# Attention inside a four-block network: score banks, exponentials and pair sums rearranged

## The chip, the cores and the metric

The kernel runs on one core of a Trainium2 chip. The metric is the device time of one execution in microseconds (us), the median over several runs.

## What is computed

The reference is a chain of blocks on 16 images of 128 channels and 32 x 32 pixels: a grouped convolution with batch normalisation, a linear attention, a compositional softmax attention, a feed-forward mixture, a second attention, and a routed mixture. The change touches only the third, which the kernel calls `phase_attn`. Cut to what matters it is

```python
sq = (x @ wq_s).reshape(b, n, S, DH).transpose(0, 2, 1, 3) * scale   # S=8 heads, DH=16, n=1024
sk = (x @ wk_s).reshape(b, n, S, DH).transpose(0, 2, 1, 3)
rv = (x @ wv_r).reshape(b, n, R, DH).transpose(0, 2, 1, 3)           # R=2
search_attn = softmax(einsum('bsid,bsjd->bsij', sq, sk), axis=-1)
retrieved = einsum('bsij,brjd->bsird', search_attn, rv)
retrieval_sim = einsum('bsid,bsird->bsir', rq, retrieved @ wk_ret)
out = einsum('bsir,bsird->bsid', softmax(retrieval_sim, -1), retrieved)
t = t + out.transpose(0, 2, 1, 3).reshape(b, n, S * DH) @ w_out
```

So there are 16 batches x 8 heads x 1024 x 1024 scores. Each gets an exponential; the exponentials are multiplied by values and also summed for the denominators.

## The kernel before

**Tiling.** For each batch, `STEPS` = 32 steps k run over query half (512 queries), quad of heads (4 of the 8) and block j of 128 keys: k = 8 g + j, with g = 2 half + quad. Step k has four scores (one per head of the quad, 128 keys x 512 queries, bf16 operands of 99 rows, L1508), four exponentials into the tile `P[k % 4]`, and four value products (L1535, float32, 32 rows of the bank `num` each, added up over the 8 steps of g). The denominators take half the products: GpSimd adds the tiles of an even step and the odd step behind it into `pairs` (L1410), and TensorE multiplies `pairs` by ones into the bank `den` (`totals`, L1546), once per two steps.

**Side work.** The scores need a maximum per query that is folded into the operands beforehand. While batch b is worked on, TensorE makes the scores of batch b+1 a second time with queries as rows (`max`, L1480, four per step) into a ring of three `side` banks, and VectorE reduces each (L1599). The same ring carries the odd jobs at fixed steps: `rows` (the maxima turned into operand rows, steps 1 and 17), `tokens` (L1492, numerators and denominators transposed to tokens, four times at steps 2 to 5 for the second half of the batch before and 18 to 21 for the first half of this one; VectorE copies them to `numT` and `recT`), `back` (steps 5 and 22) and `wout` (L1502, steps 6 and 23). `side_work(k, first, last)` returns the list of a step, odd jobs ahead of the maxima, and each unit waits until VectorE has emptied the bank three units back.

**The order on TensorE** is written out by hand, in `slot` (L1555 on). In step k: the fourth score of step k+1, the first quarter of the side work (one unit of four or five), scores 0 and 1 of step k+2 into the two-bank tile `Spair`, the middle of the side work (two units of four), on even k the totals, score 2 of step k+2 into the bank `Sone`, the rest of the side work, then the values of step k. `Sone` is one bank for scores 2 and 3, so score 3 waits until score 2's exponential is done, and score 2 of the next step until score 3's is.

**ScalarE** (`exps`, L1664 on) does one 1024-wide exponential of `Spair` (L1670) and two 512-wide ones of `Sone` (L1675) per step. At steps 8, 16, 24 and 0 of the next batch it has to empty `num` between them (`save`, L1685), and one step later `den` (L1688): `exps(b, k + 1, saved)` does it right behind the first exponential. The save of `num` waits for the last value product of the eight.

**GpSimd** (`pair`, L1405) waits for `den_done` of the pair sum before, since `pairs` is one tile, and for the exponentials of both its steps. Between pair sums it does `retrieve` in seven parts (L1411 on): behind pair sums 10 to 15 and pair sum 0 of the next batch for the first half, behind pair sums 2 to 8 for the second. Part 0 (L1423) waits for the last `tokens` of its half.

**SyncE** loads operands of later batches when the score counter `s_ready` says that a batch, or its first 24 steps, are through. The batches 0, 1, 14 and 15 are written out; 2 to 13 are a hardware loop over two batches a pass (`over`, L931).

Of the kernel before, what the change touches and what calls it, by code (L numbers as in the profile page):

```python
# [13 lines left out]
ALU = mybir.AluOpType  # L14
# [1193 lines left out]
STEPS = 32  # L1208
MAX_UNITS = 128
QUAD = 4  # L1210
SLOTS = 4
SIDES = 3
TOKENS_AT = (2, 18)
# [35 lines left out]
def phase_attn(nc, K, D, X):  # L1249
# [6 lines left out]
    with Mem(nc, "at") as m:  # L1256
        qo = [m.sb(f"qo{u}", [KM, SH, N], BF16) for u in range(2)]
        ko = [m.sb(f"ko{u}", [KM, SH, N], BF16) for u in range(2)]
        pairs = m.sb("pairs", [C, QUAD, CH])
# [3 lines left out]
        numT = [m.sb(f"numT{h}", [C, 4, 2 * C]) for h in range(2)]  # L1263
        recT = [m.sb(f"recT{h}", [C, 32]) for h in range(2)]
# [12 lines left out]
        Spair = m.ps("Spair", [C, 2, CH])  # L1277
        Sone = m.ps("Sone", [C, CH])
# [60 lines left out]
        with nc.Block() as block:  # L1339
            @block.sync  # L1340
            def _(sp):
# [31 lines left out]
                def slot(b, u, last):  # L1373
                    if not last and not is_first(b):

                        sp.wait_ge(s_ready, 96 * b)
                        load(b + 1, 1 - u, 1)
# [13 lines left out]
                    if not isinstance(b, int) or b < B - 2:  # L1391

                        sp.wait_ge(s_ready, 96 * b + 72)
                        load(b + 2, u, 0)
# [6 lines left out]
            def _(g):  # L1401
# [3 lines left out]
                def pair(b, i):  # L1405

                    wait_if(g, den_done, 16 * b + i)
                    g.wait_ge(p_ready, 96 * b + 6 * i + 6)
                    a = 2 * i % SLOTS
                    g.tensor_tensor(pairs[:, :, :], P[a][:, :, :], P[a + 1][:, :, :], ALU.add).then_inc(pair_done, 1)  # L1410

                def retrieve(b, h, part, tokens):
# [4 lines left out]
                    nv = numT[h][:, :, :].rearrange("p i (s r d) -> p (i s) r d", r=RH, d=DH)  # L1417
                    pv = prod[:, :, :].rearrange("p i (s r d) -> p (i s) r d", r=RH, d=DH)
                    rec = recT[h]
# [23 lines left out]
                    elif part == 5:  # L1443
                        step(g.tensor_tensor(heads, numT[h][:, :, :].rearrange("p i (s d) -> p (i s) d", d=DH),
# [24 lines left out]
            def _(pe):  # L1469
# [34 lines left out]
                def score(b, u, k, i, out):  # L1504
                    g, j = divmod(k, 8)
                    half, quad = divmod(g, 2)
                    h = QUAD * quad + i
                    return pe.matmul(out, ko[u][:, h, j * C:(j + 1) * C], qo[u][:, h, half * CH:(half + 1) * CH],  # L1508
                                     start=True, stop=True)

                def scores01(b, u, k):

                    wait_if(pe, p_ready, 96 * b + 3 * k - 2)
                    if k in (0, 8):
                        pe.wait_ge(row_in[u][k // 8], rows_count(b, u))
                    score(b, u, k, 0, Spair[:, 0, :])
                    score(b, u, k, 1, Spair[:, 1, :]).then_inc(s_ready, 1)

                def scores2(b, u, k):
                    wait_if(pe, p_ready, 96 * b + 3 * k)  # L1520
# [1149 lines left out]
```

## Time and profile before

| What | Value |
|---|---|
| Median of 3 runs | 5345.9 us (5343.29 to 5345.98) |
| The profiled execution: its own time | 5344.89 us |
| The profiled execution: span on the chip | 5343.3 us |
| Mean granted TensorE clock over the span | 0.908 |
| Attention phase, first score to last value product | about 2007 us |

The span is what the profiler saw of the execution, and 1.6 us lie around it. Durations below are from that one execution. PE is TensorE's matmul part, PEld its weight loads, DVE VectorE, ACT ScalarE, POOL GpSimd; a bracket at the end of a row of a timeline is the time the engine was idle before it and whose signal ended that. Matmuls overlap: one that is listed with 0.39 us gives way to the next after about 0.22 us, so starts are read, not lengths. `x8` at a value or total product is four float32 products of two passes each.

### The profile page before, as it was taken

What the parts mean: (1) busy time and instruction counts of PE and PEld (TensorE: products, weight loads), DVE (VectorE), ACT (ScalarE), POOL (GpSimd) and SP (SyncE); (2) the same over time, 40 slices, a digit from 0 to 9 for tenths busy, and PEclk for the clock granted to TensorE, in tenths of its full rate; (3) what the DMA queues carried; (4) which work ended last, traced back from release to release, by engine and by line L of the source; (5) the groups of instructions that cost most, each with busy time, mean ns of one, the idle gap of its engine ahead of it and who ended that gap; (6) DMA issues with size and microseconds to landing.
All of it is one profiled execution on the core that took longest, in us unless ns stands there. A gap on an engine that the chain in (4) does not pass through costs nothing. (4 is left out here: it accounts for less than half of the span.)

```text
span 5343.3 us, 71207 instructions
## 1 busy us (share of the span) xinstructions
PE 4422.3 (83%) x21775; PEld 1685.3 (32%) x21775; DVE 3064.3 (57%) x5454; ACT 2100.1 (39%) x3333; POOL 1821.6 (34%) x1328
## 2 busy tenths in 40 slices
PE   5499999994699999999999999976999999565323
PEld 2133333332422222222222222223444444343222
DVE  4777777764687776767677767624000000567562
ACT  3311111114526555556565555653344433413100
POOL 1000000003727776767676767772000000303001
PEclk9799999997969999999999999987999999866655
DMA  1343444424822222222222222011000000213204
GB/s 68 74 99 88 93 104 89 97 59 172 249 29 30 32 30 30 39 31 33 30 30 30 38 31 35 8 37 46 0 0 0 0 0 0 99 43 121 80 0 137
DMA packets 208208, 295.43 MB, mean 55 GB/s; under 512 B 43943, under 2 KB 136109, under 8 KB 206525
## 3 DMA queue, kind: packets, MB, share of 16 engines
q1 hardware_dynamic: 179768, 256.87, 21.7%
q10 hardware_dynamic: 23808, 25.17, 1.3%
q0 software_dynamic: 4368, 10.07, 0.6%
q8 instruction: 142, 2.33, 0.2%
q14 instruction: 122, 1.00, 0.1%
HBM read 94.49 MB, written 69.73 MB: 31 GB/s over the span
## 5 line engine op out<-in xcount | busy, mean ns | idle before, releaser
L1599 DVE TENSOR_REDUCE at_mx<-at_side 128x1 f32<-128x512 f32 x2048 | 1307.2, 686 | 387.1 <-PE at_side L1480 339.9
L1410 POOL TENSOR_TENSOR at_pairs<-at_P 128x2048 f32<-128x2048 f32 x256 | 1159.7, 4530 | 588.6 <-PE at_den L1546 475.0
L1675 ACT ACTIVATE at_P<-at_Sone 128x512 f32<-128x512 f32 x1024 | 611.5, 597 | 608.2 <-PE at_Sone L1508 607.4
L1480 PE MATMUL at_side<-at_ko,at_qo 96*128 96x512 bf16 x2048 | 716.8, 397 | 55.6 <-DMA at_ko<-qk 23.3
L1670 ACT ACTIVATE at_P<-at_Spair 128x1024 f32<-128x1024 f32 x512 | 523.7, 1023 | 217.8 <-PE at_Spair L1508 173.9
L1952 ACT ACTIVATE ff_hs<-ff_ph,ff_b 128x512 f32<-128x512 f32 x512 | 351.7, 687 | 525.0 <-PE ff_ph L1922 525.0
L1535 PE MATMUL at_num<-at_P,at_rvt 128*32 128x512 f32 x4096 | 546.7, 606 | 0.0
L1922 PE MATMUL ff_ph<-ffn_Y,ff_w 128*128 (+1 forms) x1024 | 525.3, 595 | 8.6 <-DMA ff_b<-in_b_dram 8.6
L1936 PE MATMUL ff_po<-ff_hs,ff_w2s 128*128 128x512 f32 x1024 | 522.9, 592 | 0.0
L616 PE MATMUL la_acc<-la_rep,la_wagg 128*32 128x512 f32 x4096 | 511.1, 606 | 1.1 <-DMA la_rep<-la_pad 1.1
L1971 DVE SCALAR_TENSOR_TENSOR X<-ff_po,ffn_b2w,X 128x512 f32 (+1 forms) x32 | 24.0, 751 | 823.5 <-PE ff_po L1936 823.5
L773 DVE SCALAR_TENSOR_TENSOR la_dwq<-la_pad,la_taps,la_dwq 128x1024 f32<-128x1024 f32 x384 | 491.6, 1280 | 7.2
L1508 PE MATMUL at_Sone<-at_qo,at_ko 99*128 99x512 bf16 x1024 | 399.7, 390 | 107.0 <-ACT at_P L1675 94.5
L1008 POOL TENSOR_TENSOR n_ln_ab<-n_ln_mv,eps 128x4 f32<-128x4 f32 x96 | 19.1, 199 | 1201.2 <-DVE n_ln_mv L999 1199.7
L587 POOL DMA_DIRECT2D proj<-la_y x32 | 17.4, 544 | 996.2 <-ACT la_y L847 996.2
L1508 PEld LDWEIGHTS at_Sone<-at_qo,at_ko 99*128 99x128 bf16 x1024 | 98.1, 96 | 783.9 <-ACT at_P L1675 489.8
L1480 PEld LDWEIGHTS at_side<-at_ko,at_qo 96*128 96x128 bf16 x2048 | 200.4, 98 | 372.6 <-DVE at_mx L1599 148.4
L1508 PE MATMUL at_Spair<-at_qo,at_ko 99*128 99x512 bf16 x1024 | 309.1, 383 | 0.0
L1546 PE MATMUL at_den<-at_pairs,ones 128*32 128x512 f32 x2048 | 278.0, 615 | 5.9 <-POOL at_pairs L1410 5.6
L1922 PEld LDWEIGHTS ff_ph<-ffn_Y,ff_w 128*128 128x128 f32 x1024 | 195.4, 191 | 254.2 <-issue 245.0
L1936 PEld LDWEIGHTS ff_po<-ff_hs,ff_w2s 128*128 128x128 f32 x1024 | 194.9, 190 | 245.4 <-issue 244.9
L1023 ACT ACTIVATE n_ln_xt<-n_ln_front,n_ln_ab 128x128 f32<-128x128 f32 x384 | 144.3, 456 | 103.2 <-POOL n_ln_ab L1014 93.5
(412 smaller groups left out, 4848.6 us busy)
## 6 DMA issues: line engine op xcount, KB each, us to landing
la_rep<-la_pad SPq DMA_DIRECT2D x512, 162.2 KB, 3.6
qk<-ap_part SPq DMA_DIRECT2D x32, 768.0 KB, 3.7
at_qo<-qk SPq DMA_DIRECT2D x192, 128.0 KB, 4.6
at_ko<-qk SPq DMA_DIRECT2D x192, 128.0 KB, 7.3
n_ln_xs<-X SPq DMA_DIRECT2D x96, 256.0 KB, 2.3
u<-ap_us SPq DMA_DIRECT2D x32, 320.0 KB, 4.0
X<-in_x_dram SPq DMA_DIRECT2D x4, 2048.0 KB, 21.7
proj<-la_y POOLq DMA_DIRECT2D x32, 256.0 KB, 2.3
```

Source lines behind the costliest of these rows:

```text
L616: last = pe.matmul(acc[h][32 * j:32 * j + 32, :], wagg[:, p - 1, j, g, :], view[:, :, 0:HW], start=(g == 0), stop=(g == NG - 1))
L773: v.scalar_tensor_tensor(out, image, taps[:, t:t + 1], out, ALU.mult, ALU.add).then_inc(tap_done, 1)
L1410: g.tensor_tensor(pairs[:, :, :], P[a][:, :, :], P[a + 1][:, :, :], ALU.add).then_inc(pair_done, 1)
L1480: return pe.matmul(side[bank][:, :], qo[1 - u][0:KQ, s, i * C:(i + 1) * C], ko[1 - u][0:KQ, s, h * CH:(h + 1) * CH], start=True, stop=True)
L1508: return pe.matmul(out, ko[u][:, h, j * C:(j + 1) * C], qo[u][:, h, half * CH:(half + 1) * CH], start=True, stop=True)
L1535: last = pe.matmul(num[32 * i:32 * i + 32, :], rvt[u][:, j, :], P[k % SLOTS][:, i, :], start=(j == 0), stop=(j == 7))
L1599: v.reduce_max(mx[:, n // 2, n % 2:n % 2 + 1], side[bank][:, :], AX.X).then_inc(side_saved, 1)
L1670: a.activation(P[k % SLOTS][:, 0:2, :], Spair[:, :, :], ACT.Exp).then_inc(p_ready, 1)
L1675: a.activation(P[k % SLOTS][:, 2 + i, :], Sone[:, :], ACT.Exp).then_inc(p_ready, 1)
L1922: pe.matmul(ph[j % R][:, :], w1[:, f, :], Y[:, bass.ds(b * N + half * CH, CH)], start=True, stop=True).then_inc(h_mm, 1)
L1936: done = pe.matmul(po[half][:, :], w2s[u][:, f, :], hs[j % R][:, :], start=(f == 0), stop=(f == FT - 1)).then_inc(h_used, 1)
L1952: a.activation(hs[j % R][:, :], ph[j % R][:, :], ACT.Gelu, bias=b1[:, j % FT:j % FT + 1]).then_inc(h_ready, 1)
```

## The change

The scores go into a ring `S` of three single banks, one after another: head number n = 4 k + i uses bank n % 3, and waits for the exponential of the head that had the bank before (n - 3; at the start of a batch, where the ring breaks off since 128 is not a multiple of 3, the heads one or two before). Every score raises `s_ready` and every exponential is 512 wide and raises `p_ready`, so both count 128 (`HEADS`) per batch where they counted 96. In step k TensorE now issues scores 0, 1, 2 and 3 of step k+2, each followed by a quarter of the side work, with the totals behind the second. The saves on ScalarE stand ahead of the third exponential. `pairs` becomes two tiles used in turn, so that a pair sum waits for the totals of the pair sum two back. `numT` and `recT` become one tile each, and the first copy into them waits for part 5 of the other half's `retrieve`. `tokens` move from steps 2 to 5 and 18 to 21 to steps 3 to 6 and 19 to 22. PSUM still holds eight banks (three side, three score, `num`, `den`). The diff without what only renames:

```diff
-STEPS = 32
 MAX_UNITS = 128
...
 SLOTS = 4
+STEPS = 32
 SIDES = 3
-TOKENS_AT = (2, 18)
+RING = 3
+HEADS = STEPS * 4
+TOKENS_AT = (3, 19)
 BACK_AT = (5, 22)
...
         ko = [m.sb(f"ko{u}", [KM, SH, N], BF16) for u in range(2)]
-        pairs = m.sb("pairs", [C, QUAD, CH])
+        pairs = [m.sb(f"pairs{u}", [C, QUAD, CH]) for u in range(2)]
         P = [m.sb(f"P{u}", [C, QUAD, CH]) for u in range(SLOTS)]
...
         sums = m.sb("sums", [C, 4, CH])
-        numT = [m.sb(f"numT{h}", [C, 4, 2 * C]) for h in range(2)]
-        recT = [m.sb(f"recT{h}", [C, 32]) for h in range(2)]
+        numT = m.sb("numT", [C, 4, 2 * C])
+        recT = m.sb("recT", [C, 32])
         ub = [m.sb(f"ub{h}", [C, 4, C]) for h in range(2)]
...
         side = [m.ps(f"side{u}", [C, CH]) for u in range(SIDES)]
-        Spair = m.ps("Spair", [C, 2, CH])
-        Sone = m.ps("Sone", [C, CH])
+        S = [m.ps(f"S{u}", [C, CH]) for u in range(RING)]
         num = m.ps("num", [C, CH])
...
-                        sp.wait_ge(s_ready, 96 * b)
+                        sp.wait_ge(s_ready, HEADS * b)
                         load(b + 1, 1 - u, 1)
...
-                        sp.wait_ge(s_ready, 96 * b + 72)
+                        sp.wait_ge(s_ready, HEADS * b + 96)
                         load(b + 2, u, 0)
...
-                    wait_if(g, den_done, 16 * b + i)
-                    g.wait_ge(p_ready, 96 * b + 6 * i + 6)
+                    wait_if(g, den_done, 16 * b + i - 1)
+                    g.wait_ge(p_ready, HEADS * b + 8 * i + 8)
                     a = 2 * i % SLOTS
-                    g.tensor_tensor(pairs[:, :, :], P[a][:, :, :], P[a + 1][:, :, :], ALU.add).then_inc(pair_done, 1)
+                    g.tensor_tensor(pairs[i % 2][:, :, :], P[a][:, :, :], P[a + 1][:, :, :], ALU.add).then_inc(pair_done, 1)
...
                     heads = prod[:, :, :].rearrange("p i (s d) -> p (i s) d", d=DH)
-                    nv = numT[h][:, :, :].rearrange("p i (s r d) -> p (i s) r d", r=RH, d=DH)
+                    nv = numT[:, :, :].rearrange("p i (s r d) -> p (i s) r d", r=RH, d=DH)
                     pv = prod[:, :, :].rearrange("p i (s r d) -> p (i s) r d", r=RH, d=DH)
-                    rec = recT[h]
+                    rec = recT
                     if part == 0:
...
                     elif part == 5:
-                        step(g.tensor_tensor(heads, numT[h][:, :, :].rearrange("p i (s d) -> p (i s) d", d=DH),
+                        step(g.tensor_tensor(heads, numT[:, :, :].rearrange("p i (s d) -> p (i s) d", d=DH),
                                              sim[:, :, :].rearrange("p s (r o) -> p (s r) o", o=1).to_broadcast([C, 64, DH]),
...
-                def score(b, u, k, i, out):
+                def score(b, u, k, i):
                     g, j = divmod(k, 8)
                     half, quad = divmod(g, 2)
-                    h = QUAD * quad + i
-                    return pe.matmul(out, ko[u][:, h, j * C:(j + 1) * C], qo[u][:, h, half * CH:(half + 1) * CH],
-                                     start=True, stop=True)
-
-                def scores01(b, u, k):
-
-                    wait_if(pe, p_ready, 96 * b + 3 * k - 2)
-                    if k in (0, 8):
-                        pe.wait_ge(row_in[u][k // 8], rows_count(b, u))
-                    score(b, u, k, 0, Spair[:, 0, :])
-                    score(b, u, k, 1, Spair[:, 1, :]).then_inc(s_ready, 1)
-
-                def scores2(b, u, k):
-                    wait_if(pe, p_ready, 96 * b + 3 * k)
-                    score(b, u, k, 2, Sone[:, :]).then_inc(s_ready, 1)
-
-                def scores3(b, u, k):
-                    pe.wait_ge(p_ready, 96 * b + 3 * k + 2)
-                    score(b, u, k, 3, Sone[:, :]).then_inc(s_ready, 1)
+                    h, n = QUAD * quad + i, 4 * k + i
+
+                    wait_if(pe, p_ready, HEADS * b + (n - 2 if n >= RING else n - 1 if n < 2 else -2))
+                    if k in (0, 8) and i == 0:
+                        pe.wait_ge(row_in[u][quad], rows_count(b, u))
+                    pe.matmul(S[n % RING][:, :], ko[u][:, h, j * C:(j + 1) * C], qo[u][:, h, half * CH:(half + 1) * CH],
+                              start=True, stop=True).then_inc(s_ready, 1)
...
                         wait_if(pe, num_saved, 4 * b + g)
-                    pe.wait_ge(p_ready, 96 * b + 3 * k + 3)
+                    pe.wait_ge(p_ready, HEADS * b + 4 * k + 4)
                     for i in range(QUAD):
...
                     for i in range(QUAD):
-                        last = pe.matmul(den[32 * i:32 * i + 32, :], K["ones"][:, 0:32], pairs[:, i, :],
+                        last = pe.matmul(den[32 * i:32 * i + 32, :], K["ones"][:, 0:32], pairs[(k // 2 - 1) % 2][:, i, :],
                                          start=(j == 0), stop=(j == 6))
...
                     if first:
-                        scores01(b, u, 0)
-                        scores2(b, u, 0)
-                        scores3(b, u, 0)
-                        scores01(b, u, 1)
-                        scores2(b, u, 1)
+                        for n in range(8):
+                            score(b, u, n // 4, n % 4)
                     for k in range(STEPS):
...
                         work = side_work(k, first, last)
-                        cuts = [0, (len(work) + 1) // 4, (3 * len(work) + 1) // 4, len(work)]
-                        if k + 1 < STEPS:
-                            scores3(b, u, k + 1)
-                        elif not last:
-                            scores3(b + 1, 1 - u, 0)
                         ahead_of = (b, u, k + 2) if k + 2 < STEPS else None if last else (b + 1, 1 - u, k + 2 - STEPS)
-                        for part in range(3):
-                            for w in work[cuts[part]:cuts[part + 1]]:
+                        for i in range(QUAD):
+                            if ahead_of:
+                                score(*ahead_of, i)
+                            for w in work[(i * len(work) + 2) // 4:((i + 1) * len(work) + 2) // 4]:
                                 fill(w, b, u, side_free(b, at), at % SIDES).then_inc(side_ready, 1)
                                 at += 1
-                            if part == 0 and ahead_of:
-                                scores01(*ahead_of)
-                            if part == 1 and k % 2 == 0 and not (first and k == 0):
+                            if i == 1 and k % 2 == 0 and not (first and k == 0):
                                 totals(b, k)
-                            if part == 1 and ahead_of:
-                                scores2(*ahead_of)
                         values(b, u, k)
...
                         if n == 0:
-                            wait_if(v, out_ready, 2 * b - 1 - h)
-                        v.tensor_copy(numT[h][:, n, :], side[bank][:, 0:2 * C])
-                        v.reciprocal(recT[h][:, 8 * n:8 * n + 8], side[bank][:, 2 * C::32]).then_inc(side_saved, 1)
+                            wait_if(v, post_step, 11 * (2 * b - 1 - h) + 10)
+                        v.tensor_copy(numT[:, n, :], side[bank][:, 0:2 * C])
+                        v.reciprocal(recT[:, 8 * n:8 * n + 8], side[bank][:, 2 * C::32]).then_inc(side_saved, 1)
                     elif kind == "back":
...
                         wait_if(a, pair_done, 16 * b + k // 2 - 1)
-                    a.wait_ge(s_ready, 96 * b + 3 * k + 1)
-                    a.activation(P[k % SLOTS][:, 0:2, :], Spair[:, :, :], ACT.Exp).then_inc(p_ready, 1)
-                    if saved:
-                        save(*saved)
-                    for i in range(2):
-                        a.wait_ge(s_ready, 96 * b + 3 * k + 2 + i)
-                        a.activation(P[k % SLOTS][:, 2 + i, :], Sone[:, :], ACT.Exp).then_inc(p_ready, 1)
+                    for i in range(QUAD):
+                        if saved and i == 2:
+                            save(*saved)
+                        a.wait_ge(s_ready, HEADS * b + 4 * k + i + 1)
+                        a.activation(P[k % SLOTS][:, i, :], S[(4 * k + i) % RING][:, :], ACT.Exp).then_inc(p_ready, 1)
```

## Rows read from the trace of the kernel before

**Rows 1.** The page, busy time of each engine over the whole span.
```profile
PE 4422.3 (83%) x21775; PEld 1685.3 (32%) x21775; DVE 3064.3 (57%) x5454; ACT 2100.1 (39%) x3333; POOL 1821.6 (34%) x1328
```

**Rows 2.** Stretches, busy us (count) of PE, PEld, DVE, ACT, POOL, then TensorE clock, DMA.
```profile
1544.00:3551.60 2007.60, 1865.80 (x10838) 537.05 (x10837) 1383.58 (x2410) 1191.44 (x1756) 1444.38 (x626) 0.99 0.20 29
2339.40:2464.60 125.20, 117.97 (x690) 34.44 (x690) 92.09 (x161) 74.90 (x111) 91.28 (x41) 1.00 0.23 32
```

**Rows 3.** The page, costliest groups: the attention's own on DVE, POOL and ACT.
```profile
L1599 DVE TENSOR_REDUCE at_mx<-at_side 128x1 f32<-128x512 f32 x2048 | 1307.2, 686 | 387.1 <-PE at_side L1480 339.9
L1410 POOL TENSOR_TENSOR at_pairs<-at_P 128x2048 f32<-128x2048 f32 x256 | 1159.7, 4530 | 588.6 <-PE at_den L1546 475.0
L1675 ACT ACTIVATE at_P<-at_Sone 128x512 f32<-128x512 f32 x1024 | 611.5, 597 | 608.2 <-PE at_Sone L1508 607.4
...
L1670 ACT ACTIVATE at_P<-at_Spair 128x1024 f32<-128x1024 f32 x512 | 523.7, 1023 | 217.8 <-PE at_Spair L1508 173.9
```

**Rows 4.** Timeline of TensorE, steps 28 and 29 of a batch.
```profile
2542.94 0.39 PE L1508 MATMUL at_Sone<-at_qo,at_ko 99*128 99x512 bf16 x1
...
2543.38 0.60 PE L1508 MATMUL at_Spair<-at_qo,at_ko 99*128 99x512 bf16 x2
...
2544.34 1.06 PE L1546 MATMUL at_den<-at_pairs,ones 128*32 128x512 f32 x8
2545.34 0.39 PE L1508 MATMUL at_Sone<-at_qo,at_ko 99*128 99x512 bf16 x1
...
2545.88 1.07 PE L1535 MATMUL at_num<-at_P,at_rvt 128*32 128x512 f32 x8
2546.88 0.39 PE L1508 MATMUL at_Sone<-at_qo,at_ko 99*128 99x512 bf16 x1
...
2548.72 1.07 PE L1535 MATMUL at_num<-at_P,at_rvt 128*32 128x512 f32 x8
2549.72 0.39 PE L1508 MATMUL at_Sone<-at_qo,at_ko 99*128 99x512 bf16 x1
```

**Rows 5.** Timeline, end of step 7 and start of step 8.
```profile
2464.59 1.07 PE L1535 MATMUL at_num<-at_P,at_rvt 128*32 128x512 f32 x8
2465.80 0.58 ACT L1685 COPY at_sums<-at_num 128x512 f32<-128x512 f32 x1 [0.95 <-PE at_num L1535]
...
2466.28 0.60 ACT L1675 ACTIVATE at_P<-at_Sone 128x512 f32<-128x512 f32 x1
...
2466.94 0.39 PE L1508 MATMUL at_Sone<-at_qo,at_ko 99*128 99x512 bf16 x1 [1.28 <-ACT at_P L1675]
```

**Rows 6.** Waits of TensorE over the whole attention: us in total, times, longest.
```profile
PE at_Sone L1508 <- ACT at_P L1675: 94.5, 73, 6.5
```

**Rows 7.** Timeline, steps 5 and 6 of a batch, which carry the odd jobs.
```profile
2453.57 0.60 PE L1492 MATMUL at_side<-ident,at_sums 128*128 128x128 f32 x4
...
2454.55 0.20 DVE L1628 RECIPROCAL at_recT<-at_side 128x8 f32<-128x8 f32 x1
...
2456.56 2.36 POOL L1423 TENSOR_TENSOR at_prod<-at_numT,at_ub 128x1024 f32<-128x1024 f32 x1
2456.75 1.06 PE L1535 MATMUL at_num<-at_P,at_rvt 128*32 128x512 f32 x8
...
2459.27 1.02 PE L1480 MATMUL at_side<-at_ko,at_qo 96*128 96x512 bf16 x3
```

**Rows 8.** Timeline, last batch: two pair sums, and two scores through one bank.
```profile
3538.29 4.53 POOL L1410 TENSOR_TENSOR at_pairs<-at_P 128x2048 f32<-128x2048 f32 x1 [0.36 <-PE at_den L1546]
...
3544.05 4.54 POOL L1410 TENSOR_TENSOR at_pairs<-at_P 128x2048 f32<-128x2048 f32 x1 [0.26 <-PE at_den L1546]
...
3545.19 0.39 PE L1508 MATMUL at_Sone<-at_qo,at_ko 99*128 99x512 bf16 x1
...
3546.27 0.39 PE L1508 MATMUL at_Sone<-at_qo,at_ko 99*128 99x512 bf16 x1 [0.26 <-ACT at_P L1675]
```

**Rows 9.** Timeline of TensorE, first instruction of a new pass of the batch loop.
```profile
2562.26 0.60 PE L1508 MATMUL at_Sone<-at_qo,at_ko 99*128 99x512 bf16 x1 [5.70 <-issue]
```

## The prediction

> **What bounds the kernel now.** I read the page first: TensorE is busy 83% of the span, the other engines 34 to 57% [rows 1]. The chain that ended last is the tail of the last block and says nothing of the attention, so I cut that phase out: 2007.6 us, in which TensorE is busy 1865.80, VectorE 1383.58, GpSimd 1444.38, ScalarE 1191.44, at a granted clock of 0.99, the level of 2.4 GHz [rows 2]. One batch is 125.20 us. No engine but TensorE is near its limit, and the large idle times of the others behind it (608.2 us of ScalarE before scores, 475.0 of GpSimd before totals [rows 3]) are theirs, not the kernel's. So the question is where TensorE stands still.
>
> The timeline answers it. From start to start, an even and an odd step without odd jobs take 2546.88 - 2542.94 = 3.94 us and 2549.72 - 2546.88 = 2.84 us [rows 4]. A score or maximum gives way after 0.22, a value or total product after 1.00, and each change to float32 costs some 0.09: 8 x 0.22 + 1.00 + 0.09 = 2.84 and 1.09 more for the totals. These steps have no stall. At 32 steps they would make 16 x 6.78 = 108.5 us; the odd jobs (8 `tokens` and 2 `back` at 0.44, 2 `wout` at 0.86, 2 `rows` at 0.22) about 6.6 more. That is 115.1 of 125.2, so only some 10 us per batch are open at all.
>
> More than half of it is the save of `num`. Values of step 7 start at 2464.59, so the next score could start at 2465.59. ScalarE has to wait for these values, saves at 2465.80, starts the exponential behind it at 2466.28, and only its end frees `Sone`: the score starts at 2466.94, 1.35 us late [rows 5]. Four of these per batch are 5.4 us. The wait of TensorE on this line is 94.5 us in the phase [rows 6]. The rest are `rows` (twice 1.3, bound by VectorE's chain of four) and steps with `tokens`, `back` and `wout`.
>
> **The ring and the saves.** The work of TensorE stays: the same 2048 scores in a phase of 512 steps, the same side units, the same products. What moves is the order. After the change step 7 issues all of step 9's scores, of which two exponentials stand before the save and two behind it. Step 8 begins with the score of head 40, which needs the exponential of head 37: done before the save. A maximum follows, then at 0.44 head 41, which needs the exponential of head 38, the first behind the save. That ends at the same moment as now, so head 41 starts 1.35 after the step's start: stall 0.91 instead of 1.35 [rows 5]. The second exponential behind it starts one rhythm of 0.48 later (save to exponential in rows 5), long before its bank is wanted behind the totals. Gain 0.44 each, not 1.35. Of the 64 saves, 1 has no successor, 5 fall on the loop's turn, where TensorE stands 5.70 us for its own instructions [rows 9], and 3 are in the last batch (below): 55 x 0.44 = 24.2 us.
>
> **The exponentials.** The split costs ScalarE 2 x 597 - 1023 = 171 ns per step [rows 3], 88 us in all, bringing its 1191 to about 1280 of 2007 [rows 2]: hidden, and the end moves by nothing. What counts is latency. One bank passed on from score to score takes 1.08 us (3545.19 to 3546.27) [rows 8]. In the ring the closest pair is head 0 and head 3 of an odd step: 3 scores, 3 maxima between starts, 6 x 0.22 = 1.31. That is exactly the distance at which score 3 and score 2 stand now in the odd step that has no stall [rows 4]. Margin 0.23; if this cover were gone, each 0.1 us would cost 25.6 over 256 odd steps. The row's slope is (1023 - 597)/512 = 0.83 ns an element and leaves 0.17 us fixed. The Trainium skill (ScalarE: Activation LUTs, Rules for kernel authors) budgets about 0.3 us per activation plus 0.83 ns per element. By that estimate the exponential would be 0.72 and the bank's passage 1.21, still under 1.31: the margin would shrink and the sum stay.
>
> **One more wait and one more signal per step on TensorE.** Score 0 had no signal, score 1 no wait. Maxima, which have both, and the pair of scores, which has them once, keep the same 0.22 [rows 4], so I take 0; the upper bound is 0.09, the gap that a change to float32 shows, 46 us over 512 steps. The Trainium skill (TensorE: Matmul & The Clock Gate, The cost: per-tile semaphore tail) speaks against the change: an increment on every matmul serialises at about 26 ns. By it the estimate would be 512 x 26 ns = 13 us less gain; no row shows such a step.
>
> **Two pair tiles.** GpSimd may start a pair sum when both steps' exponentials are there, half a us before the even step, instead of behind its totals, about 3 us earlier. TensorE waits for it nowhere in the loop, so this gives 0 there. What it covers: part 0 of `retrieve` now waits for `tokens` in step 6 or 22. Token start to reciprocal's end is 1.18 (2453.57 to 2454.75) and part 0 takes 2.36 [rows 7]: in step 6, 0.22 + 1.18 + 0.1 + 2.36 = 3.9, then the pair sum of 4.53 [rows 3] ends at 8.4. Steps 6 (3.94 + 0.44 + 0.86) and 7 take 5.24 + 2.84 = 8.08, and the exponential that overwrites its tile is queued behind the save, at 9.7; totals at 9.9. Slack over 1 us, cost 0. In step 22 the slack is larger, with `back` and `wout` in the steps.
>
> **Moved odd jobs.** `tokens` move by one step; two of each half stay in odd steps. Step 5 (`tokens`, `back`) is bound by VectorE's emptying now, 3.18 us from tokens to values (2453.57 to 2456.75) [rows 7]; with the last maxima spread out I get 3.01. In step 6 the third maximum of a row of three waits 0.20 for `wout`'s bank (1.02 instead of 0.82 [rows 7]); in the new order it comes behind the totals. With some 0.1 elsewhere, 0.5 per batch x 14 = 7.0 us; bounds 0 and 14. The single `numT` waits for part 5, which ends a step and more before. SyncE's thresholds mark the same heads; queue waits there cost 0.
>
> **The last batch** has no maxima. Its pair sums follow each other at 5.76 (3538.29 to 3544.05) [rows 8]: sum, totals, sum, one tile. With two it is TensorE: odd step 1.08 + 0.22 + 1.09 = 2.39, even 3.94 - 4 x 0.22 = 3.06, 5.45 in all. 15 x 0.31 less GpSimd's `retrieve`, which then nearly fills it: 3 us, bounds 0 and 8.
>
> **Sum.** 24.2 + 7.0 + 3 = 34. The profiled execution is 5344.9, so 5311; the median is 1.0 above it: 5312.
>
> **Rivals.**
> 1. The save's stall goes wholly, because the score that waits finds other work ahead of it. For: the ring has one bank more ahead. Against: TensorE issues in order and head 41 is third in its row. 5346 - 55 x 1.35 - 10 = 5262. Chance 0.06.
> 2. The ring gains nothing: the stall is only moved, the jobs' gain is eaten by waits on `tokens`, within 10 us of 5346. For: the order is new in all 512 steps. Chance 0.13.
> 3. Slower: the passage of a bank from head 0 to head 3 in odd steps is longer than 1.31, since ScalarE's four small exponentials run closer behind one another. Price 256 us per us over; it decides from 1.31 + 34/256 = 1.44 on. At 1.54 it is 59 - 34 = 25 slower, 5371. For: margin 0.23 only. Against: 1.08 measured, and the same distance stands unstalled today. Chance 0.12.
> 4. The added wait and signal do cost something on TensorE, a part of the gap of 0.09: at 0.03 a step 15 us, so 5327, still faster. For: no row has four signalled scores in a step. Against: signalled maxima keep 0.22. Chance 0.09. The page's rule on increments, above, is this mechanism at its own price.
> The forecast itself, 5300 to 5322: 0.60.
>
> **Numbers.** Faster by over 0.2% (under 5335; 10.7 us is about what can be told from no change): 0.60 + 0.06 + 0.09 = 0.75; within: 0.13; slower: 0.12. The range leaves out rival 1 and rival 3: 5280 to 5350.
>
> **What would show it.** TensorE's wait on the scores at steps 8, 16, 24 and 0 about 0.9, between the first maximum and the second score; these steps 4.85 instead of 5.29; clean steps still 3.94 and 2.84; GpSimd's wait for totals gone; pairs in the last batch under 5.76. Wrong would be odd steps above 2.84, TensorE waiting for pair sums at steps 8 or 24, or ScalarE waiting for them.

## The result and the profile after

The changed kernel takes 5306.68 us (median of 4, 5304.48 to 5312.56) against 5345.34 for the one before: a ratio of 0.993, with a 95% interval of 0.9917 to 0.9943. It is 38.7 us faster; 34 were forecast and the range held.

The page of the changed kernel, busy time and the attention's groups (the columns as in [rows 3]):

```profile
PE 4422.0 (83%) x21774; PEld 1678.8 (32%) x21775; DVE 3041.7 (57%) x5454; ACT 2105.6 (40%) x3845; POOL 1822.3 (34%) x1328
...
L1652 ACT ACTIVATE at_P<-at_S 128x512 f32<-128x512 f32 x2048 | 1120.2, 599 | 749.5 <-PE at_S L1513 698.1
L1411 POOL TENSOR_TENSOR at_pairs<-at_P 128x2048 f32<-128x2048 f32 x256 | 1160.3, 4533 | 316.1 <-ACT at_P L1652 295.5
```

The stretch from the first score to the last value product (columns as in [rows 2]):

```profile
1544.00:3516.70 1972.70, 1870.26 (x10833) 530.27 (x10832) 1361.35 (x2409) 1193.81 (x2263) 1446.35 (x626) 0.98 0.21 29
```

The busy times beside [rows 1] and [rows 2] are nearly the same: 1865.80 and 1870.26 us of TensorE, 1444.38 and 1446.35 of GpSimd. What became shorter is the time in which TensorE stands. GpSimd's wait for totals, 475.0 us in [rows 3], is gone from its row, and that by itself says nothing of the time, as the experiments show.

Waits of TensorE in the changed kernel, without the end of the last batch (total, times, longest; `DVEq` is the part of VectorE that issues its instructions); the first line answers to [rows 6]:

```profile
PE at_S L1513 <- ACT at_P L1652: 76.0, 77, 5.4
PE at_side L1481 <- DVEq L1601: 13.0, 29, 0.5
```

94.5 us have become 76.0. The timeline at the end of step 7 and the start of step 8, which answers to [rows 5], shows where:

```profile
2321.09 1.06 PE L1524 MATMUL at_num<-at_P,at_rvt 128*32 128x512 f32 x8
2322.09 0.39 PE L1513 MATMUL at_S<-at_qo,at_ko 99*128 99x512 bf16 x1
2322.30 0.59 ACT L1662 COPY at_sums<-at_num 128x512 f32<-128x512 f32 x1 [1.54 <-PE at_num L1524]
...
2323.44 0.39 PE L1513 MATMUL at_S<-at_qo,at_ko 99*128 99x512 bf16 x1 [0.74 <-ACT at_P L1652]
...
2323.98 1.06 PE L1535 MATMUL at_den<-at_pairs,ones 128*32 128x512 f32 x8
```

Step 8 begins at 2322.09 without a wait. The second score starts at 2323.44, 1.35 us behind it, as the stalled score in [rows 5] did; but a score and a maximum have been issued meanwhile. The late moment is the same, but more of the row's work has been issued before it, so 0.44 us less of TensorE's time is lost.

For the rest I took from the timelines of both kernels the start of every group of value products (L1535 before, L1524 after). The distance between two of them is the length of a step. The median over six batches away from the loop's turn, in us:

| Steps | Before | After |
|---|---|---|
| clean odd, clean even | 2.84, 3.94 | 2.85, 3.95 |
| 8 and 24; 16 | 5.29; 5.21 | 4.86; 4.78 |
| 1 to 6 together | 26.16 | 25.36 |
| 17 to 23 together | 28.87 | 28.40 |
| last batch, 31 steps | 94.4 | 95.3 |
| turn of the loop, over a clean batch (mean of 5) | 6.7 | 9.1 |

From the first to the last value product the profiled executions take 1998.4 and 1967.2 us: the attention gave 31.2 of the 38.7. The remainder is outside. The first value product starts at 1552.18 in the profile before and 1547.67 in the one after, and over the profiles of all kernels of this study, which share every line up to there, it moves between 1543.7 and 1552.2. The last two rows of the table took back some 13 us: 5 turns at 2.4, and 0.9 in the last batch.

### The profile page after: what moved, and what is told of

Read it like the earlier page. It is cut to its first block and busy times, and to the rows that moved or that the text cites. A ratio compares the mean times of both kernels' runs of the same rounds, so it can differ in the third digit from the quotient of the medians.

```text
span 5305.1 us, 72474 instructions
## 1 busy us (share of the span) xinstructions
PE 4422.0 (83%) x21774; PEld 1678.8 (32%) x21775; DVE 3041.7 (57%) x5454; ACT 2105.6 (40%) x3845; POOL 1822.3 (34%) x1328
## 5 line engine op out<-in xcount | busy, mean ns | idle before, releaser
L1652 ACT ACTIVATE at_P<-at_S 128x512 f32<-128x512 f32 x2048 | 1120.2, 599 | 749.5 <-PE at_S L1513 698.1
L1513 PE MATMUL at_S<-at_qo,at_ko 99*128 99x512 bf16 x2048 | 784.2, 387 | 76.0 <-ACT at_P L1652 76.0
L1481 PE MATMUL at_side<-at_ko,at_qo 96*128 96x512 bf16 x2048 | 788.8, 398 | 44.0 <-DMA at_ko<-qk 23.3
L1524 PE MATMUL at_num<-at_P,at_rvt 128*32 128x512 f32 x4096 | 550.1, 609 | 0.0
L1513 PEld LDWEIGHTS at_S<-at_qo,at_ko 99*128 99x128 bf16 x2048 | 196.1, 97 | 884.0 <-ACT at_P L1652 684.2
L1535 PE MATMUL at_den<-at_pairs,ones 128*32 128x512 f32 x2048 | 277.1, 613 | 7.7 <-POOL at_pairs L1411 7.6
L616 PEld LDWEIGHTS la_acc<-la_rep,la_wagg 128*32 128x32 f32 x4096 | 105.8, 108 | 246.5 <-issue 228.1
L831 ACT COPY la_agg<-la_acc 128x512 f32<-128x512 f32 x64 | 37.5, 587 | 343.1 <-PE la_acc L616 343.1
```

The lines of the kernel that those rows point to most:

```text
L616: last = pe.matmul(acc[h][32 * j:32 * j + 32, :], wagg[:, p - 1, j, g, :], view[:, :, 0:HW], start=(g == 0), stop=(g == NG - 1))
L1481: return pe.matmul(side[bank][:, :], qo[1 - u][0:KQ, s, i * C:(i + 1) * C], ko[1 - u][0:KQ, s, h * CH:(h + 1) * CH], start=True, stop=True)
L1513: pe.matmul(S[n % RING][:, :], ko[u][:, h, j * C:(j + 1) * C], qo[u][:, h, half * CH:(half + 1) * CH], start=True, stop=True).then_inc(s_r ...
L1524: last = pe.matmul(num[32 * i:32 * i + 32, :], rvt[u][:, j, :], P[k % SLOTS][:, i, :], start=(j == 0), stop=(j == 7))
L1535: last = pe.matmul(den[32 * i:32 * i + 32, :], K["ones"][:, 0:32], pairs[(k // 2 - 1) % 2][:, i, :], start=(j == 0), stop=(j == 6))
L1652: a.activation(P[k % SLOTS][:, i, :], S[(4 * k + i) % RING][:, :], ACT.Exp).then_inc(p_ready, 1)
```

## The experiments

Each kernel differs from the changed kernel or from the one before by the lines shown. The ratio is that to runs of the kernel before taken beside them, with its 95% interval. Those runs had medians of 5342.4 to 5343.9, against 5345.34 beside the changed kernel, so a difference in time to the changed kernel is good to some 3 us; the lengths of steps are steadier.

**1. The save one exponential earlier** (save_second).

```diff
-                        if saved and i == 2:
+                        if saved and i == 1:
```

> The changed kernel with one edit: ScalarE saves num and den ahead of the second exponential of the four instead of the third. Theory A (the stall at steps 8, 16, 24 and 0 is the score whose bank is emptied by the first exponential behind the save; its size is 1.35 us less the place of that score in TensorE's row): that score is then the first of the row (place 0 instead of 0.44), so these steps go from 4.86 back to about 5.29 and the time from 5306.7 to 5306.7 + 55 x 0.44 = 5331. Rival B (the changed kernel gained there because exponentials are shorter and the totals stand earlier, wherever the save is): no change, 5307.

Measured 5338.69 (5334.56 to 5341.4), ratio 0.9989 (0.9979 to 0.9999). Steps 8 and 24 take 5.35, steps 16 and 32 5.28; nothing else in a clean batch moved. Its timeline at step 8:

```profile
2330.29 1.06 PE L1524 MATMUL at_num<-at_P,at_rvt 128*32 128x512 f32 x8
2331.50 0.59 ACT L1662 COPY at_sums<-at_num 128x512 f32<-128x512 f32 x1 [2.03 <-PE at_num L1524]
...
2332.64 0.39 PE L1513 MATMUL at_S<-at_qo,at_ko 99*128 99x512 bf16 x1 [1.28 <-ACT at_P L1652]
```

The first score of step 8 now waits, 1.35 us from 2331.29 again. Nearly the whole gain of the change is gone, with ring, pair tiles and narrow exponentials all in place. Rival B falls. The loss is 32.0 us where 24 were expected: the save steps are 0.49 longer instead of 0.43, and the last batch, which I had left out, is 2.1 longer.

**2. The save one exponential later** (save_fourth).

```diff
-                        if saved and i == 2:
+                        if saved and i == 3:
```

> The changed kernel with one edit: ScalarE saves num and den ahead of the fourth exponential. Theory A: the score that waits for it is then the third of the row, behind the totals (place 1.96, after the 1.35), so the stall goes wholly: steps 8, 16, 24 and 0 fall from 4.86 to 3.94, and the time to 5306.7 - 55 x 0.91 = 5257. Rival B (what stands behind the save is late anyhow, so another wait takes the place): less than a third of it, over 5290.

Measured 5267.24 (5265.57 to 5271.72), ratio 0.986 (0.9844 to 0.9877): 39.4 us less than the changed kernel. The save steps take 3.94 and 3.95, and 4.06 at step 32. The timeline at step 8 has the same save and no stall:

```profile
2302.05 1.07 PE L1524 MATMUL at_num<-at_P,at_rvt 128*32 128x512 f32 x8
2303.05 0.39 PE L1513 MATMUL at_S<-at_qo,at_ko 99*128 99x512 bf16 x1
2303.26 0.59 ACT L1662 COPY at_sums<-at_num 128x512 f32<-128x512 f32 x1 [1.06 <-PE at_num L1524]
...
2303.49 0.38 PE L1513 MATMUL at_S<-at_qo,at_ko 99*128 99x512 bf16 x1
...
2304.02 1.06 PE L1535 MATMUL at_den<-at_pairs,ones 128*32 128x512 f32 x8
```

Of the expected 50, 39.4 came. Clean batches lost 3.1 us each, but at the turn of the loop a batch costs 10.3 over a clean one instead of 9.1, and step 10 has become 0.18 longer.

**3. The totals earlier instead of the save later** (totals_first).

```diff
-                            if i == 1 and k % 2 == 0 and not (first and k == 0):
+                            if i == 0 and k % 2 == 0 and not (first and k == 0):
```

> The changed kernel with one edit: on even steps the totals stand behind the first score and its maximum instead of behind the second. Theory A: head 1 of the row is then at place 1.5, past the 1.35, so the stall of 0.91 at the four save steps goes as it does in save_fourth, though the save stays where it is: 5257. It needs the pair sum 0.44 us plus earlier; the trace has it ready by 0.2 us or more at step 8. Rival B: the pair sum is late at steps 8 and 24 and TensorE waits for it instead, 5280 or more. Rival C (ScalarE itself is what is late): 5307.

Measured 5281.2 (5278.7 to 5282.43), ratio 0.9885 (0.9868 to 0.9901). Steps 8 and 24 fall to 3.98 and 3.95 though the save was not touched, so theory A holds for these steps a third time, from TensorE's side. The time is not the 5257 of theory A, though, but the one named for rival B, whose mechanism came at other steps: TensorE's waits of that kernel now have a line for pair sums.

```profile
PE at_S L1513 <- ACT at_P L1652: 31.1, 9, 5.6
...
PE at_den L1535 <- POOL at_pairs L1411: 10.0, 28, 1.3
```

They are at steps 10 and 26 (4.42 and 4.25 instead of 3.94), behind the second part of `retrieve`, not at 8 and 24. Steps 4, 6, 20 and 22 are 0.09 longer each as well.

**4. The unit `rows` behind the maxima** (rows_last).

```diff
-        if k == ROWS_AT[1]:
-            work.append(("rows", 1))
...
-        if k == ROWS_AT[0]:
-            work.append(("rows", 0))
         work += [("max", n) for n in range(QUAD * k, QUAD * k + QUAD)]
+        if k == ROWS_AT[0]:
+            work.append(("rows", 0))
+    if post and k == ROWS_AT[1]:
+        work.append(("rows", 1))
```

> The changed kernel with one edit: at steps 1 and 17 the unit rows stands behind the four maxima instead of ahead of them. Theory A (these steps take 4.3 us instead of 3.1 because VectorE's chain of four holds one of three side banks and VectorE itself, with four maxima behind it): the chain then runs beside the value products, and both steps fall by about 1.1: 5306.7 - 2 x 1.1 x 14 = 5276. Rival B (the chain is only moved into the next step, whose maxima then wait): no change, 5307.

Measured 5280.12 (5277.57 to 5280.85), ratio 0.988 (0.9864 to 0.9897). Steps 1 and 17 fall from 4.39 to 3.10; the next step is 0.18 longer. The wait on `DVEq` above, 29 times, is not in this kernel's list. Rival B is right for 0.18 of 1.29.

**5. The place of the save in the kernel before** (old_save_last).

```diff
-                    if saved:
-                        save(*saved)
                     for i in range(2):
+                        if saved and i == 1:
+                            save(*saved)
```

> The kernel before, with its double bank and its single one, and one edit: ScalarE saves num and den ahead of the third exponential (the second 512-wide one) instead of the second. Theory A (the place of the save alone makes the stall, the ring is not needed for it): the score that waits for the exponential behind the save is then the third of the next row, behind the totals, so steps 8, 16, 24 and 0 fall from 5.3 to 3.94 and the time by 55 x 1.3 = 72 from 5345: 5273, well under the changed kernel. Rival B (one single bank for two scores can't take a save without the ring): the save delays the fourth score instead, over 5320.

Measured 5274.32 (5269.24 to 5278.86), ratio 0.9869 (0.9853 to 0.9886). Steps 8, 16 and 24 take 3.94. This one edit of the old kernel is worth 68 us, more than the whole change:

```profile
2311.31 1.06 PE L1535 MATMUL at_num<-at_P,at_rvt 128*32 128x512 f32 x8
2311.47 0.59 ACT L1675 ACTIVATE at_P<-at_Sone 128x512 f32<-128x512 f32 x1
2312.31 0.39 PE L1508 MATMUL at_Sone<-at_qo,at_ko 99*128 99x512 bf16 x1
2312.52 0.58 ACT L1685 COPY at_sums<-at_num 128x512 f32<-128x512 f32 x1 [0.46 <-PE at_num L1535]
```

The exponential that frees `Sone` has started before the save, and the score at 2312.31 does not wait. The ring was not needed to take this stall away, and as built it took away a third of it.

**6. One pair tile in the changed kernel** (one_pair_tile). The tile, its wait (`16 * b + i`) and its uses are those of the kernel before.

```diff
-        pairs = [m.sb(f"pairs{u}", [C, QUAD, CH]) for u in range(2)]
+        pairs = m.sb("pairs", [C, QUAD, CH])
...
-                    wait_if(g, den_done, 16 * b + i - 1)
+                    wait_if(g, den_done, 16 * b + i)
```

> The changed kernel with one tile for the pair sums instead of two, each sum waiting for the totals of the sum before. Theory A (the second tile buys nothing in the loop): clean steps and save steps as in the changed kernel (2.85, 3.94, 4.86), only the last batch 3 us longer: 5307 to 5310. Rival B (the second tile is what lets the moved tokens and the pair sums stand side by side): TensorE waits at steps 8, 10, 24 and 26, over 5320.

Measured 5312.3 (5308.73 to 5317.36), ratio 0.9941 (0.9925 to 0.9958). The time lies between the two forecasts, 5.6 us above the changed kernel. All steps of a clean batch agree with the changed kernel within 0.02, and the last batch takes 97.5 instead of 95.3. Rival B falls: in the steps of the loop the second tile is worth nothing, and in the last batch 2.2 us.

**7. The other half of the change alone, in the kernel before** (old_two_pairs). Two pair tiles, one `numT` and `recT`, `tokens` at 3 and 19, with the old banks, order and exponentials.

```diff
-TOKENS_AT = (2, 18)
+TOKENS_AT = (3, 19)
...
-                    wait_if(g, den_done, 16 * b + i)
+                    wait_if(g, den_done, 16 * b + i - 1)
```

> The kernel before, its score banks, order on TensorE and exponentials as they were, with the other half of the change alone: two pair tiles, one numT and recT, tokens one step later. Theory A (this half is worth nothing in the loop): 5340 to 5350, save steps still 5.3, with GpSimd's wait for totals gone. Rival B (it is worth part of the 39 us): under 5335.

Measured 5341.4 (5334.54 to 5342.45), ratio 0.9993 (0.9984 to 1.0003): no difference. GpSimd's largest waits in it:

```profile
POOL at_pairs L1410 <- ACT at_P L1675: 356.0, 126, 88.2
POOL at_prod L1423 <- DVE at_recT L1628: 141.7, 31, 4.8
```

The 475 us of waiting for totals of [rows 3] have become waiting for exponentials and for `tokens`. GpSimd was not what the loop waited for; only the name of its releaser changed. The steps say that two small things cancel in the time: steps 1 to 6 and 17 to 23 fall by 0.36 per batch together, and the last batch rises from 94.4 to 97.1.

**8. `tokens` back at 2 and 18 in the changed kernel** (tokens_early).

```diff
-TOKENS_AT = (3, 19)
+TOKENS_AT = (2, 18)
```

> The changed kernel with tokens back at steps 2 and 18. Steps 2 to 6 and 18 to 23 became 0.8 and 0.45 us shorter per batch in the changed kernel. Theory A (that comes from the order in a step, scores between the side units): the sum of these steps stays within 0.1 per batch, and the last batch is 3 us shorter, since GpSimd no longer waits 4.6 us for tokens there: 5303. Rival B (it comes from the move): 1.0 per batch is lost, 5320.

Measured 5299.73 (5294.63 to 5306.39), ratio 0.9917 (0.99 to 0.9933). Steps 1 to 6 and 17 to 23 together take 53.63 against 53.76 (55.03 before the change), so what these steps gained comes from the order within a step. With `tokens` at the same steps as in the kernel before, it lies at steps 3, 5 and 6 (0.21, 0.43 and 0.21) and 19, 21 and 22 (0.21, 0.21 and 0.09). The last batch takes 89.6 instead of 95.3. GpSimd's waits in the last batch, first the changed kernel, then this one:

```profile
POOL at_prod L1424 <- DVE at_recT L1607: 7.6, 2, 4.6
```

```profile
POOL at_prod L1424 <- DVE at_recT L1607: 0.6, 2, 0.4
```

**9. The 1024-wide exponential split, alone, in the kernel before** (old_split).

```diff
-                    a.activation(P[k % SLOTS][:, 0:2, :], Spair[:, :, :], ACT.Exp).then_inc(p_ready, 1)
+                    a.activation(P[k % SLOTS][:, 0, :], Spair[:, 0, :], ACT.Exp)
+                    a.activation(P[k % SLOTS][:, 1, :], Spair[:, 1, :], ACT.Exp).then_inc(p_ready, 1)
```

> The kernel before with one edit: the 1024-wide exponential of the double bank as two 512-wide ones behind one another, with the same waits and the same signal behind the second. Theory A (the narrower exponentials are hidden and follow one another at 0.49 us, so that ScalarE's busy time hardly grows): clean steps stay 2.84 and 3.94, ScalarE's busy time in the phase 1190 to 1210, time within 5 us of 5342. Rival B (four exponentials per step cost on the path, 0.17 us each): odd steps over 2.9. On the turn of the batch loop: it cost the old order 6.9 us over a clean batch and the ring 9.1. If that comes from the longer list of instructions on ScalarE, it is 8 or more here, and the time 5 to 8 us longer; if it comes from TensorE's order or its waits, 6.9 stays.

Measured 5344.68 (5338.12 to 5349.43), ratio 1.0002 (0.9993 to 1.0012). All steps as before. The stretch of the attention:

```profile
1544.00:3551.00 2007.00, 1864.39 (x10837) 536.68 (x10835) 1383.31 (x2409) 1222.26 (x2265) 1445.76 (x626) 0.99 0.20 29
```

ScalarE has some 510 more instructions and 31 us more busy time than in [rows 2], a little over the 1190 to 1210 expected. The turn of the loop costs 6.8 us, so four exponentials a step instead of three are not what made it 9.1. This kernel still has three waits and three signals per step on ScalarE, where the ring has four.

**10 and 11. Together.** `save_fourth_rows_last` has the edits of 2 and 4, `three_edits` that of 8 as well.

> The changed kernel with both edits, the save ahead of the fourth exponential and rows behind the maxima. They gave 39.4 and 26.6 us alone and lie in different steps: if they add up, 5306.7 - 66 = 5241. If GpSimd or VectorE becomes the bound in between, less: over 5250.

> The changed kernel with three edits: save ahead of the fourth exponential, rows behind the maxima, tokens at steps 2 and 18. The first two together gave 5227.7; tokens_early shortened the last batch from 95.3 to 89.6 us. If that holds here too: 5222. If rows at step 1 and tokens at step 2 get into each other's way (the step behind rows is 0.18 longer already): 5227 or more.

Measured 5227.73 (5227.58 to 5231.53), ratio 0.9787 (0.9771 to 0.9804), and 5219.48 (5217.62 to 5223.82), ratio 0.977 (0.9754 to 0.9786). The first is 13 us better than the sum of its parts. By the steps the parts just add up: a clean batch falls by 5.4, and by 3.1 and 2.3 with each alone. The phase falls by 75.6 (1967.2 to 1891.6) against 40.7 + 30.7 = 71.4, so most of the 13 lies outside the attention. In the second the step behind `rows` is 4.56 long, 0.18 over one with `tokens` alone, and the last batch 88.2. It is the fastest of all, 87 us under the changed kernel.

**12. The two edits in the kernel before** (old_save_rows), those of 5 and 4.

> The kernel before with its double bank, and two edits: the save ahead of the third exponential and rows behind the maxima. The first gave 68 us. Theory A (rows is VectorE's chain, the same in both orders): 1.1 us less at steps 1 and 17, 27 to 34 less than 5274: 5240 to 5247. Against 5227.7 of the ring with the same two edits, the ring's own order would be worth 12 to 20 us. Rival B (with three maxima in one row the chain is in the way again): over 5260.

Measured 5254.71 (5245.9 to 5258.84), ratio 0.9832 (0.9815 to 0.9848). Steps 1 and 17 fall to 3.15, but the step behind them rises from 4.40 to 4.92, so half a microsecond of 1.24 comes back: neither theory is wholly right. A clean batch takes 118.8 against 117.0 of the ring with the same two edits. What is left of the change beside these two edits is worth 1.8 us per batch; in the times it is 27 us, of which the phase, first to last value product, shows 20.9 (1912.5 against 1891.6). Since the split exponentials (9) and the second pair tile (6, 7) gave nothing in the loop's steps, these 1.8 are the ring with its order and the moved `tokens`. Against `three_edits`, which has `tokens` at the same steps as this kernel, it is 2.1 per batch and 35 us in the times.

## Why the prediction was right

**Where TensorE stands** was read rightly: clean steps at 2.84 and 3.94 have no stall, and but for steps 10 and 26 in experiments 2, 3 and 10 they kept their length to 0.01 in every kernel of the study. One reading was wrong without harm to the sum: the gap of 0.09 is not that of a change to float32. In the trace before, value products, totals and `rows` (32 columns of weights, `128*32`) start 0.31 to 0.32 us behind a score or maximum, but the float32 products of `tokens`, `back` and `wout` (`128*128`) 0.22 to 0.23, like a bf16 one.

**The saves** were the term that carried the sum, 55 x 0.44 = 24.2. The steps gave 0.43 each, and a stall of 0.91 was left, as forecast, at the place forecast. That the stall is 1.35 less the place of the waiting score is shown by moving the save both ways (1, 2), by moving the totals (3) and in the old order (5).

**The exponentials** were right in cost (9: nothing). A term beside the sum was wrong: I let ScalarE's busy time grow by 88 us; it grew by 2. Two 512-wide exponentials behind one another are listed at 1.09 us, not at twice 0.60, so a row's mean length is not what one of a series costs. The estimate from the Trainium skill (ScalarE: Activation LUTs, Rules for kernel authors) of 0.72 for one was not what the trace showed: 0.599. The page's 0.3 us is for an activation whose bias is an operand in memory, and these have none.

**The added wait and signal** cost nothing that a step shows: 2.85 against 2.84, at most 0.01 x 512 = 5 us. By the figure of the Trainium skill (TensorE: Matmul & The Clock Gate, The cost: per-tile semaphore tail) I had estimated 0.026; the page gives it as a tail behind matmuls that each increment a semaphore, and used as a cost per step it is not borne out. The step lengths leave nothing of rival 4.

**Two pair tiles** were right at 0 in the loop (6, 7).

**The moved jobs** were put at 0.5 per batch and gave 0.80 + 0.47 = 1.27: the mechanism was right and the size too small. I worked out step 5 as 0.17 and it gave 0.44. I had followed only one side bank. My reading, which no run separates, is that with the even spacing VectorE has emptied a bank before it is wanted again. That the move itself is not the cause is shown by 8, where these steps gain 1.40 without it; in the old order the move gives 0.36 (7).

**The last batch** was the step that failed: `+3`, measured -0.9. I let GpSimd's `retrieve` nearly fill it and did not ask what the later `tokens` do there. Part 0 waits for them 4.6 us, and with no maxima between the scores the steps are too short to make that up. The slack that I worked out for step 22 held in the loop and not here. Experiment 8 shows it: 5.7 us; in the old order it is 2.7 (7). The second tile by itself was worth 2.2 here (6), so the term forecast was about right and a cost beside it was put at nothing. The sign that I had named, pair sums less than 5.76 apart, came only in part: undisturbed ones start down to 4.50 us apart, but at the two waits for `tokens` 9.96 and 11.55 us, where it was 6.95 before, and the mean rose from 6.25 to 6.35.

**The turn of the loop** I let lose its own gain only, 5 x 0.44 = 2.2. It costs 2.4 us more per pass than before, 12 in all. TensorE's own gap there did not grow: it is 4.75 to 5.40 us in the five turns, and was 5.21 to 6.54. What grew lies behind it. Around the third turn, first before, then after the change:

```profile
2555.50 1.07 PE L1535 MATMUL at_num<-at_P,at_rvt 128*32 128x512 f32 x8
...
2559.97 0.58 ACT L1685 COPY at_sums<-at_num 128x512 f32<-128x512 f32 x1
```

```profile
2537.91 1.94 PE L1524 MATMUL at_num<-at_P,at_rvt 128*32 128x512 f32 x8
...
2539.92 0.59 ACT L1662 COPY at_sums<-at_num 128x512 f32<-128x512 f32 x1 [2.53 <-PE at_num L1524]
...
2541.12 0.61 PE L1513 MATMUL at_S<-at_qo,at_ko 99*128 99x512 bf16 x1 [1.27 <-ACT at_P L1652]
```

Before, TensorE had issued the values of the last step when it stood still (its next start is that of [rows 9]), so ScalarE saved `num` within the gap and the stall of this save was hidden. In the ring the score that waits for ScalarE's turn stands ahead of these values; they come behind the gap, the save behind them, and TensorE waits a second time, 1.27 to 1.67 us in the five turns, where before it had no such wait. The clock stays low longer too. Over the 11 us from TensorE's restart the granted clock was 0.70 to 0.80 before and is 0.53 to 0.65 after; the third turn again, before and after (columns as in [rows 2]):

```profile
2562.26:2573.26 11.00, 10.23 (x45) 2.61 (x46) 6.18 (x12) 4.92 (x7) 5.77 (x2) 0.78 0.13 16
```

```profile
2536.95:2547.95 11.00, 9.73 (x40) 2.08 (x41) 3.86 (x7) 5.46 (x11) 5.76 (x2) 0.65 0.18 26
```

That is a stretch at 0.50, which is 1.2 GHz, of 4.3 to 6.7 us before (5.4 in the mean) and 7.8 to 10.4 after (9.0). As an estimate from these numbers: 0.7 less in the gap, 1.4 for the second wait, half of the 2.2 us by which the stretch is longer without that wait, and the 0.4 that the save gained elsewhere and not here, 2.2 of the 2.4. With the save moved the turn is 10.3 in the ring (2), where the second wait is still there (1.36 to 1.79), and 8.7 in the old order (5), where there is none. Experiment 9 rules out the number of exponentials. No run moves the waiting score behind the values of the last step, so this account rests on the traces alone. Why ScalarE itself stands longer at its turn, 6.04 to 6.68 us against 4.21 to 5.47 before, stays open.

These two misses, 3.9 and 9.8 us, were made up by the jobs' larger gain (17.8 instead of 7.0), so that the phase gave 31.2 of the 34 forecast; the other 7 of the measured 38.7 lie outside it and belong to no step of mine. The total was nearer than its parts, and that was luck: the save was sized rightly, and four errors of 4 to 11 us nearly cancelled.

**The rivals.** Rival 1 (the stall goes wholly) is false for this change. Rival 2 and rival 3 fall by the steps.

## What to carry to other kernels

Where an in-order engine waits once in a while for a chain through another engine, write down the moment at which the chain ends and the place of the waiting instruction in its row; the stall is the difference. Moving one instruction was worth at least as much here as another bank: 39 us for the save and 25 for the totals, against some 24 that the ring took from the saves. An idle row of an engine that isn't the bound, like GpSimd's 475 us, may vanish without a gain that the time shows; look at the step lengths, and price a moved job in the shortest step it will meet, here the last batch.

## What the hardware showed that was not expected

Back-to-back exponentials of 128x512 from single banks start 0.49 us apart and are listed at 0.60 each; groups of two at 1.09, of four at 2.07.

At the turn of the batch loop in the changed kernel ScalarE stands 6.04 us with no wait that the profile shows, and TensorE behind it 4.75, before TensorE has come to its own turn:

```profile
2536.30 1.09 ACT L1652 ACTIVATE at_P<-at_S 128x512 f32<-128x512 f32 x2 [6.04 <-issue]
2536.95 0.61 PE L1513 MATMUL at_S<-at_qo,at_ko 99*128 99x512 bf16 x1 [4.75 <-ACT at_P L1652]
```

ScalarE stood at its turn before the change as well, 4.21 to 5.47 us. TensorE's own stand ended later there, so that two of its five gaps are put down to its own instructions, like that of [rows 9]; after the change all five are put down to ScalarE. The granted clock behind this gap of 4.75 us was 0.50, which is 1.2 GHz, for 7.85 us (columns as in [rows 2]):

```profile
2536.95:2544.80 7.85, 6.58 (x22) 1.10 (x22) 2.30 (x4) 3.21 (x6) 3.23 (x1) 0.50 0.25 37
```

So a turn costs TensorE twice, in the gap and in the slow stretch behind it, and in the ring a third time, in the second wait described above. With the save moved in the old order the turn is nearly all that is left of TensorE's waits for its scores:

```profile
PE at_Sone L1508 <- issue: 33.4, 5, 7.2
```
